# A fused transformer block on one core: down products three slots behind, and another order of the attention's steps

## The chip, the cores and the metric

The kernel runs on 1 core of one Trainium2 chip. The time is the device time in microseconds (us) of one launch, the median of 3 runs. A profiled execution of its own gives the trace; its time stands below beside the span of the trace. The engines are called PE (TensorE), DVE (VectorE), ACT (ScalarE), POOL (GpSimd) and SP (SyncE, which here only starts transfers).

## The reference

Four residual steps on x of 16 batches of 128 tokens by 128 features, in fp32:

```python
x = x + diffusion(x, zX, zY, zR)                    # two 3-point laplacians and zR * x * (1 - x)
x = x + moe(x, probs, shared_prob, Wg, Wu, Wd, Sg, Su, Sd)
#   8 dense experts and a shared one, F = 512: down(silu(x @ Wg) * (x @ Wu)), weighted by the batch's gates
x = x + lora(x, language_ids, A, B, embed)          # rank 16
x = x + attention(x, side, lengths, Wq..., bo)
#   16 heads of 8; 128 keys of the side input under a length mask, and one key of the token's own
```

## The kernel before, in words

**First phase: the experts.** The 16 batches are done in 4 tiles of 4 batches, so that a tile is 128 features by 512 tokens. A tile has 36 **slots**: 9 experts (the shared one is the ninth) by 4 chunks of 128 of the 512 hidden units. Slot k is: `gate_product` (g_ps), `up_product` (u_ps), and `down_product` of an earlier slot into acc_ps, which sums over all 36. Each product is three 128x512 matmuls (line 520 to 522), since every fp32 operand is split into a high and a low fp32r part: high by high, high by low, low by high. Between up and down the chunk goes through four steps: `silu` on ACT (act_p from g_ps, line 818), `product` on DVE (act_p times u_ps, line 1097), `round_act` on ACT (act_hi, line 823), `split_act` on DVE (act_lo = act_p - act_hi, line 1101). The order on each engine is written out by hand. ACT's slot k is silu of k, then round of k - 1; DVE's is product of k, then split of k - 1; PE's is gate of k, up of k, an auxiliary step if the slot has one, down of k - 2. act_p, act_hi and act_lo have three buffers each; g_ps and u_ps three banks each, so that gate k waits for silu k - 3 and up k for product k - 3.

The gates are applied to the input of the up product: for each expert POOL makes xg (line 1299) and xg_lo (line 1303), ACT xg_hi (line 828). In the first tile the weights are loaded and split too: SP loads w_raw (three buffers, three parts per expert), ACT rounds it (line 789), POOL subtracts (line 1292). **Auxiliary steps** lie in fixed slots of PE and drain on DVE or ACT one slot later. `FIRST_SLOT` lists those of the first tile: bias in slot 4, setup (two small transposes of the lora matrices) in 5, side in 6, query in 8, four natural projections in 10 to 16, and the next tile's from 18 on. A natural step has a product on POOL (`multiply_self`, line 1308, one slot later) and a sum on DVE (`sum_self`, line 1061, two slots later). After a query step SP writes q_rows to memory in six transfers of 128 KB, on the same queue as the weights. `add_experts` (line 1106) adds acc_ps to x1 in slot 1 of the next tile, and `later_step` runs lora, key and value for the tile before. The last tile's later steps are done in the first bodies of the attention.

**Second phase: the attention**, one `body` per batch b, in pairs of batches whose blocks SP loads (`load_first`: k_blocks and q_plain; `load_second`: q_blocks and k_plain; about 768 KB each). The scores are computed twice: `scores` (s_ps, queries on partitions), only to take each token's maximum on DVE (`max_group`, line 1169, then `merge_max`, line 1177); and `scores_t` (st_ps, keys on partitions) for the exponentials on ACT (line 931), where the maximum goes in as two extra rows of q_blocks. The maximum gets there in this way: POOL's `split_max` (lines 1360 to 1365) makes neg_max, PE's `turn_max` (line 595) transposes it, ACT's `copy_max` (line 883) copies it to max_rows, and POOL's `place_max` (line 1351) starts a transfer into q_blocks, which `scores_t` waits for. Then `weigh` (probabilities by values), `take_pv` on ACT, `turn_pv`, `normalise` on DVE, `turn_attn`, `copy_attn` on ACT, `project`, `make_out` on DVE, and the store on SP, one transfer per pair. PE's body b is, in this order:

```python
for i in range(2):
    scores(b + 2, n + 2, i)
    scores_t(b, n, i)
weigh(b - 1, n - 1, 0); weigh(b - 1, n - 1, 1)
turn_attn(b - 2, n - 2)
scores(b + 2, n + 2, 2); scores(b + 2, n + 2, 3)
scores_t(b, n, 2)
weigh(b - 1, n - 1, 2); weigh(b - 1, n - 1, 3)
project(b - 2, n - 2)
scores_t(b, n, 3)
turn_pv(b - 1, n - 1)
turn_max(b + 2, n + 2)
```

SP's `step(p)` starts load_first of pair p + 2, then load_second of pair p + 1 once the maximum of batch 2p + 1 is placed (`max_placed[1]`), then the store of pair p - 3; before step 2 it stores the k_rows of the last tile.

## Time and profile before

| | us |
|---|---|
| median of 3 runs | 474.82 |
| lowest, highest | 471.68, 476.14 |
| the profiled execution's own time | 470.62 |
| its span, first to last instruction | 468.8 |
| PE busy | 432.4 |
| DVE, ACT, POOL busy | 334.4, 282.0, 185.5 |

The profiled execution took 1.8 us more than its span, and 4.2 us less than the median. The span has these stretches: up to 8.07 the start; 8.07 to 113.87 the first tile, with the weights; 113.87 to 370.80 the three other tiles; from there the attention, in which 370.80 to 399.01 holds bodies 0 to 3 with the last tile's later steps, and 454.46 to 468.80 the last two bodies and the end. Matmuls are pipelined, and the profile models their ends: two that start 0.23 us apart are each shown as 0.39 us long. So a late start of less than 0.16 us does not show as idle time.

### The profile page before, as it was taken

The numbers are of one execution on the slowest core, as the hardware profiler recorded it, in microseconds if no ns is written. First come the engines' busy times: TensorE is split into PE (matmuls) and PEld (weight loads), VectorE is DVE, ScalarE is ACT, GpSimd is POOL, SyncE is SP. The second block draws the span as 40 slices with busy tenths as digits, with TensorE's granted clock in tenths as the row PEclk, the third lists the DMA queues.
The fourth block names the chain that finished last, engine by engine and source line by source line (L and its number), as shares of the span: only waits on it lengthen the run. The fifth ranks groups of instructions, "written<-read, shape, count | busy, mean of one in ns | idle before, by whom it ended". The sixth has DMA issues, their size and how long they took to land.

```text
span 468.8 us, 7759 instructions
## 1 busy us (share of the span) xinstructions
PE 432.4 (92%) x2280; PEld 324.5 (69%) x2280; DVE 334.4 (71%) x589; ACT 282.0 (60%) x572; POOL 185.5 (40%) x235
## 2 busy tenths in 40 slices
PE   7799699699999999999999999999999977988896
PEld 3568578578678787867878787788788554554453
DVE  4887467586777779777767987686687757567763
ACT  5757367575465657645565755555555646567684
POOL 0857567573223222332224222334377324234440
PEclk9999799899999999999999999999999989789999
DMA  5524214210002020000111000001221714665630
GB/s 161 157 74 149 91 52 129 78 37 3 1 1 90 1 68 1 22 0 0 53 36 35 32 0 1 1 27 42 69 70 34 171 50 122 175 156 148 152 104 24
DMA packets 27891, 30.69 MB, mean 65 GB/s; under 512 B 4276, under 2 KB 22296, under 8 KB 27864
## 3 DMA queue, kind: packets, MB, share of 16 engines
q1 hardware_dynamic: 26664, 29.99, 22.5%
q0 software_dynamic: 768, 0.28, 0.3%
q8 instruction: 12, 0.20, 0.2%
q10 hardware_dynamic: 432, 0.10, 0.1%
q14 instruction: 15, 0.12, 0.1%
HBM read 22.73 MB, written 7.35 MB: 64 GB/s over the span
## 4 chain that ended last, share of the span: by engine, by line
PE 59%; DVE 14%; issue 9%; DMA 6%; ACT 6%; POOL 5%; POOLq 1%; DVEq 0%; ACTq 0%; SPq 0%
PE acc_ps L520 7%; DVE act_lo L1101 6%; PE g_ps L520 5%; PE acc_ps L521 5%; PE g_ps L522 5%; PE g_ps L521 5%; PE acc_ps L522 5%; PE u_ps L520 5%; PE u_ps L522 5%; PE u_ps L521 5%; DVE act_p L1097 4%; DMA w_raw<-in_L_cond_Wu 4%; ACT act_p L818 2%; DMA squares<-in_squares 1%; DMA q_blocks<-max_rows 1%
## 5 line engine op out<-in xcount | busy, mean ns | idle before, releaser
L818 ACT ACTIVATE act_p<-g_ps 128x512 f32<-128x512 f32 x144 | 86.0, 597 | 127.9 <-PE g_ps L522 112.4
L1097 DVE TENSOR_TENSOR act_p<-act_p,u_ps 128x512 f32<-128x512 f32 x144 | 98.5, 684 | 71.4 <-PE u_ps L522 45.7
L1101 DVE TENSOR_TENSOR act_lo<-act_p,act_hi 128x512 fp32r<-128x512 f32 x144 | 122.8, 853 | 0.2 <-ACT act_hi L823 0.2
L1303 POOL TENSOR_TENSOR xg_lo<-xg,xg_hi 128x512 fp32r<-128x512 f32 x35 | 49.6, 1418 | 155.1 <-ACT xg_hi L828 155.1
L823 ACT ACTIVATE act_hi<-act_p 128x512 fp32r<-128x512 f32 x144 | 89.8, 624 | 2.0 <-DVE act_p L1097 1.8
L520 PE MATMUL acc_ps<-act_hi,w_split 128*128 128x512 f32 x144 | 62.0, 431 | 15.9 <-DVE act_lo L1101 15.8
L520 PE MATMUL g_ps<-x_hi,w_split 128*128 128x512 f32 (+1 forms) x144 | 57.6, 400 | 0.6 <-DVE x_lo L1130 0.6
L521 PE MATMUL acc_ps<-act_lo,w_split 128*128 128x512 f32 x144 | 57.1, 397 | 0.0
L522 PE MATMUL acc_ps<-act_hi,w_split 128*128 128x512 f32 x144 | 56.9, 395 | 0.0
L520 PE MATMUL u_ps<-xg_hi,w_split 128*128 128x512 f32 x144 | 56.8, 394 | 0.1
L521 PE MATMUL g_ps<-x_lo,w_split 128*128 128x512 f32 (+1 forms) x144 | 56.8, 394 | 0.0
L522 PE MATMUL g_ps<-x_hi,w_split 128*128 128x512 f32 (+1 forms) x144 | 56.8, 394 | 0.0
L521 PE MATMUL u_ps<-xg_lo,w_split 128*128 128x512 f32 x144 | 56.7, 393 | 0.0
L522 PE MATMUL u_ps<-xg_hi,w_split 128*128 128x512 f32 x144 | 56.6, 393 | 0.0
L1292 POOL TENSOR_TENSOR w_split<-w_raw,w_split 128x512 fp32r<-128x512 f32 x26 | 38.1, 1469 | 34.6 <-ACT w_split L789 34.6
L520 PEld LDWEIGHTS acc_ps<-act_hi,w_split 128*128 128x128 f32 x144 | 27.4, 190 | 34.1 <-DVE act_lo L1101 22.1
L1169 DVE TENSOR_REDUCE max_key<-s_ps 128x4 f32<-128x512 f32 x56 | 36.6, 686 | 16.2 <-PE s_ps L588 15.6
L1299 POOL TENSOR_TENSOR xg<-x,gates 128x512 f32 (+1 forms) x35 | 39.2, 1121 | 5.0 <-ACT x L798 2.8
L688 PE MATMUL st_ps<-q_blocks,k_plain 98*128 98x512 f32 x64 | 29.8, 471 | 3.5 <-DMA q_blocks<-max_rows 3.0
L520 PEld LDWEIGHTS g_ps<-x_hi,w_split 128*128 128x128 f32 x144 | 27.4, 190 | 7.1 <-DVE x_lo L1130 1.4
L520 PEld LDWEIGHTS u_ps<-xg_hi,w_split 128*128 128x128 f32 x144 | 27.3, 190 | 6.6 <-issue 0.5
L522 PEld LDWEIGHTS acc_ps<-act_hi,w_split 128*128 128x128 f32 x144 | 27.5, 191 | 6.1
(190 smaller groups left out, 679.8 us busy)
## 6 DMA issues: line engine op xcount, KB each, us to landing
k_blocks<-k_rows SPq DMA_DIRECT2D x32, 96.0 KB
q_plain<-q_rows SPq DMA_DIRECT2D x8, 384.0 KB
q_blocks<-q_rows SPq DMA_DIRECT2D x32, 96.0 KB
k_plain<-k_rows SPq DMA_DIRECT2D x8, 384.0 KB
w_raw<-in_L_cond_Wg SPq DMA_DIRECT2D x8, 256.0 KB, 2.7
w_raw<-in_L_cond_Wu SPq DMA_DIRECT2D x8, 256.0 KB, 2.7
w_raw<-in_L_cond_Wd SPq DMA_DIRECT2D x8, 256.0 KB, 2.9
q_rows<-rows_hi SPq DMA_DIRECT2D x16, 128.0 KB
```

Of the source, the lines that this page charges most:

```text
L520: mm(dst, w_h, x_h, start=start, stop=False)
L521: mm(dst, w_h, x_l, start=False, stop=False)
L522: return mm(dst, w_l, x_h, start=False, stop=stop)
L688: mm(st_ps[i % 2][:], k_plain[n // 2 % 2][0:ROWS + 2, i, half(n)], q_blocks[n // 2 % 2][0:ROWS + 2, :, i, half(n)], start=True, stop=True) ...
L818: activation(act_p[k % 3][:], g_ps[k % 3][:], ACT.Silu).then_inc(silu_done, 1)
L823: activation(act_hi[k % 3][:], act_p[k % 3][:], ACT.Identity).then_inc(act_hi_done, 1)
L1097: tt(act_p[k % 3][:], act_p[k % 3][:], u_ps[k % 3][:], ALU.mult).then_inc(prod_done, 1)
L1101: tt(act_lo[k % 3][:], act_p[k % 3][:], act_hi[k % 3][:].bitcast(F32), ALU.subtract).then_inc(act_lo_done, 1)
L1169: nc.vector.tensor_reduce(max_key[n % 2][:, i], (s_ps[i % 2] if bank is None else bank)[:].rearrange("p (j s) -> p j s", j=GJ), AX_X, ALU. ...
L1292: tt(w_lo[:, w // 3, w % 3], w_raw[w % 3][:], w_hi[:, w // 3, w % 3].bitcast(F32), ALU.subtract)\
L1299: tt(xg[:], x1[:, t], over_s(gates[:, e, bass.ds(t * TB, TB)]), ALU.mult).then_inc(xg_made, 1)
L1303: tt(xg_lo[e % 3][:], xg[:].rearrange("p b s -> p (b s)"), xg_hi[e % 3][:].bitcast(F32), ALU.subtract)\
```

## The change

Two things, and a few moves that go with them.

**Experts.** Down products lie three slots behind (`BEHIND = 3`) in place of two. act_hi and act_lo get four buffers (`ACTS = 4`), and act_p lies in the same memory as act_lo, so that `split_act` works in place; `silu` of k now waits for down k - 4 in place of split k - 3. `add_experts` moves from slot 1 to slot 2. In the first tile setup moves from slot 5 to slot 17; `sum_self` comes four slots after its natural step in place of two, and POOL's `multiply_self` at the start of the second slot in place of the end of the first. `select_language`, a small copy, is taken out of `later_step` to ahead of its wait. In the last slot of the last tile ACT rounds 34 before silu 35, and DVE splits 34 before product 35.

**Attention.** The body has both next scores first, then `turn_max(b + 1)`, then both transposed scores. `turn_max` of a batch is thus in the body after the one that took its maximum. ACT's `copy_max` and `exp_self` move along to the start of the body, and POOL's `place_max` comes ahead of `weigh_self`, with `pick_mask` ahead of it. A `first_body` mixes the last three down products with the first scores. The last two bodies have values, take_pv and copy_attn on DVE in place of ACT. The last pair is stored as two transfers; the other stores are where they were.

```diff
-FIRST_SLOT = {4: ("bias", 0, 0), 5: ("setup", 0, 0), 6: ("side", 0, 0), 8: ("query", 0, 0)}
+FIRST_SLOT = {4: ("bias", 0, 0), 6: ("side", 0, 0), 8: ("query", 0, 0)}
+FIRST_SLOT |= {17: ("setup", 0, 0)}
+ACTS = 4
+BEHIND = 3
...
-        act_p = [sb(f"act_p{n}", [128, N]) for n in range(3)]
-        act_hi = [sb(f"act_hi{n}", [128, N], F32R) for n in range(3)]
-        act_lo = [sb(f"act_lo{n}", [128, N], F32R) for n in range(3)]
+        act_hi = [sb(f"act_hi{n}", [128, N], F32R) for n in range(ACTS)]
+
+        with ExitStack() as products:
+            act_p = [products.enter_context(nc.sbuf_tensor(f"act_p{n}", [128, N], F32)) for n in range(ACTS)]
+        act_lo = [sb(f"act_lo{n}", [128, N], F32R) for n in range(ACTS)]
...
-                if p >= 3:
-                    store_out(p - 3)
+                if 3 <= p < NP + 2:
+                    store_out((p - 3) * PAIR, (p - 2) * PAIR)
...
+            for b in range(B - PAIR, B):
+                store_out(b, b + 1)
...
-                down_product(*((t, k - 2) if k >= 2 else (t - 1, SLOTS - 2 + k)))
+                down_product(*((t, k - BEHIND) if k >= BEHIND else (t - 1, SLOTS - BEHIND + k)))
...
+            def first_body():
+
+                down_product(NT - 1, SLOTS - 3)
+                pe.wait_ge(silu_done, NT * SLOTS - 1)
                 for i in range(2):
-                    if s_next:
+                    scores(2, 2, i)
+                down_product(NT - 1, SLOTS - 2)
+                pe.wait_ge(silu_done, NT * SLOTS)
+                for i in range(2):
+                    scores_t(0, 0, i)
+                down_product(NT - 1, SLOTS - 1)
+                for i in range(2, GI):
+                    scores(2, 2, i)
+                last_tile_step(0, 1)
+                scores_t(0, 0, 2)
+                last_tile_step(0, 2)
+                scores_t(0, 0, 3)
+
+            def body(b, n, s_next=True, turn_next=True):
+
+                if s_next:
+                    for i in range(2):
                         scores(b + 2, n + 2, i)
+                if turn_next:
+                    turn_max(b + 1, n + 1)
+                for i in range(2):
                     scores_t(b, n, i)
...
-                if s_next:
-                    turn_max(b + 2, n + 2)
...
             def silu(t, k):
-                wait(act, act_lo_done, t * SLOTS + k - 2)
+                wait(act, down_done, t * SLOTS + k - 3)
...
             def round_act(t, k):
-                wait(act, down_done, t * SLOTS + k - 2)
+                wait(act, down_done, t * SLOTS + k - 3)
...
-            def body(b, n, s_next=True):
+            def body(b, n):
+                if n:
+                    copy_max(b + 1, n + 1)
                 exp_scores(b, n, 0)
+                if n:
+                    exp_self(b + 1, n + 1)
                 exp_scores(b, n, 1)
...
-                for kind, f, b in first_at(k - 2):
+                for kind, f, b in first_at(k - 4):
                     if kind == "natural":
                         sum_self(f, b)
...
-                if k == 1:
+                if k == BEHIND - 1:
                     add_experts(t - 1)
...
+            def last_body(b):
+                place_values(b, b)
+                copy_attn(b - 2, b - 2)
+                take_pv(b - 1, b - 1)
+                make_out(b - 2, b - 2)
+                normalise(b - 1, b - 1)
...
             def pick_mask(b, n):
-                nc.gpsimd.tensor_copy(mask_col[n % 4][:], mask_cols[:, bass.ds(b, 1)]).then_inc(mask_picked, 1)
+                pool.wait_ge(max_copied, b + 1)
+                tt(mask_col[n % 4][:], mask_cols[:, bass.ds(b, 1)], warm[:, 0:1], ALU.add).then_inc(mask_picked, 1)
...
-            def body(b, n, s_next=True):
+            def body(b, n, s_next=True, place_next=True):
+                if n and place_next:
+                    pick_mask(b + 1, n + 1)
+                    place_max(b + 1, n + 1)
+                weigh_self(b, n)
                 if s_next:
                     split_max(b + 2, n + 2)
```

## Rows read from the trace of the kernel before

**Rows 1.** Windows by stage: stretch, length, busy times, granted clock, DMA share, GB/s.

```profile
8.07:113.87 105.80, 92.61 (x398) 72.45 (x399) 76.72 (x137) 67.00 (x128) 66.22 (x54) 0.95 0.31 90
113.87:200.13 86.26, 85.12 (x386) 68.62 (x385) 66.13 (x103) 50.95 (x95) 25.09 (x24) 1.00 0.08 25
...
370.80:399.01 28.21, 21.99 (x169) 12.89 (x167) 19.38 (x40) 15.89 (x39) 9.47 (x32) 0.93 0.38 98
399.01:454.46 55.45, 49.13 (x460) 29.01 (x460) 38.22 (x89) 37.72 (x99) 19.23 (x67) 0.91 0.57 152
```

**Rows 2.** Waits of PE, whole span: total us, times, longest us.

```profile
PE acc_ps L520 <- DVE act_lo L1101: 15.8, 17, 3.9
PE max_ps L595 <- POOL neg_max L1363: 7.7, 11, 2.9
PE st_ps L688 <- DMA q_blocks<-max_rows: 3.0, 3, 2.0
```

**Rows 3.** Timeline of PE, first tile: start, length, instruction, [idle before, releaser].

```profile
51.35 0.39 PE L522 MATMUL u_ps<-xg_hi,w_split 128*128 128x512 f32 x1
55.59 0.80 PE L520 MATMUL acc_ps<-act_hi,w_split 128*128 128x512 f32 x1 [3.86 <-DVE act_lo L1101]
...
91.00 0.54 PE L520 MATMUL acc_ps<-act_hi,w_split 128*128 128x512 f32 x1 [3.73 <-DVE act_lo L1101]
```

**Rows 4.** Timeline of the other engines in the first long wait.

```profile
51.36 0.63 ACT L789 ACTIVATE w_split<-w_raw 128x512 fp32r<-128x512 f32 x1 [3.78 <-DMA w_raw<-in_L_cond_Wu]
...
53.72 1.27 POOL L1303 TENSOR_TENSOR xg_lo<-xg,xg_hi 128x512 fp32r<-128x512 f32 x1
53.78 0.38 DVE L1061 TENSOR_REDUCE self_score<-stage 128x16 f32<-128x128 f32 x1 [5.01 <-POOL stage L1308]
```

**Rows 5.** Windows of the first tile with a granted clock of 0.50.

```profile
53.80:60.60 6.80, 5.01 (x12) 3.99 (x13) 4.60 (x10) 2.98 (x6) 4.05 (x4) 0.50 0.23 77
91.40:94.70 3.30, 3.30 (x9) 2.47 (x8) 3.30 (x7) 1.46 (x4) 1.13 (x2) 0.50 0.27 79
```

**Rows 6.** Timeline of PE, second tile: down products of three slots that follow one another.

```profile
129.64 0.39 PE L520 MATMUL acc_ps<-act_hi,w_split 128*128 128x512 f32 x1
...
131.68 0.39 PE L520 MATMUL acc_ps<-act_hi,w_split 128*128 128x512 f32 x1
...
134.12 0.51 PE L520 MATMUL acc_ps<-act_hi,w_split 128*128 128x512 f32 x1 [0.24 <-DVE act_lo L1101]
```

**Rows 7.** Timeline of DVE there: the split for the third of them.

```profile
132.51 1.56 DVE L1101 TENSOR_TENSOR act_lo<-act_p,act_hi 128x512 fp32r<-128x512 f32 x1
```

**Rows 8.** Timeline of PE from the last down products to the last tile's key.

```profile
368.91 0.50 PE L520 MATMUL acc_ps<-act_hi,w_split 128*128 128x512 f32 x1 [0.78 <-DVE act_lo L1101]
...
378.10 0.39 PE L595 MATMUL max_ps<-squares,neg_max 128*32 128x128 f32 x1 [2.87 <-POOL neg_max L1363]
...
380.90 0.63 PE L522 MATMUL out_ps<-in_hi,w_qkv_l 128*128 128x512 f32 x1
```

**Rows 9.** Timeline of PE in the loop of the attention.

```profile
427.73 0.28 PE L595 MATMUL max_ps<-squares,neg_max 128*32 128x128 f32 x1 [0.49 <-POOL neg_max L1363]
...
434.29 0.49 PE L688 MATMUL st_ps<-q_blocks,k_plain 98*128 98x512 f32 x1 [0.41 <-DMA k_plain<-k_rows]
...
438.89 0.28 PE L595 MATMUL max_ps<-squares,neg_max 128*32 128x128 f32 x1 [0.58 <-POOL neg_max L1363]
...
443.73 0.28 PE L595 MATMUL max_ps<-squares,neg_max 128*32 128x128 f32 x1 [0.49 <-POOL neg_max L1363]
```

**Rows 10.** Timeline of POOL and of SP there, and max_rows' tile view, last line.

```profile
429.23 0.63 POOL L1351 DMA_DIRECT2D q_blocks<-max_rows  x1
...
428.28 1.52 SPq L454 DMA_DIRECT2D q_blocks<-q_rows  x4
429.84 0.35 SPq L458 DMA_DIRECT2D k_plain<-k_rows  x1
...
DMA to landing us min/median/max: 2.3/3.9/7.1
```

More of the change, by code:

```diff
@@ L627, in down_product @@
                 pe.wait_ge(act_lo_done, t * SLOTS + k + 1)
-                last = three(acc_ps[:], w_hi[:, e, 2, chunk], w_lo[:, e, 2, chunk], act_hi[k % 3][:], act_lo[k % 3][:],
+                last = three(acc_ps[:], w_hi[:, e, 2, chunk], w_lo[:, e, 2, chunk], act_hi[k % ACTS][:], act_lo[k % ACTS][:],
                              start=(k == 0), stop=(k == SLOTS - 1))
@@ L677, in _ @@
                     turn_max(EARLY_TURN[k], EARLY_TURN[k])
-            for k in range(2):
-                down_product(NT - 1, SLOTS - 2 + k)
             def scores_t(b, n, i):
@@ L751, in body @@
                     turn_pv(b - 1, n - 1)
[L752 to L755 removed]
+            first_body()
             body(1, 1)
@@ L886, in last_slots @@
                 for k in range(LAST_ROUND, SLOTS):
-                    silu(t, k)
-                    round_act(t, k - 1)
+                    if k == SLOTS - 1 and not rounds_next:
+                        round_act(t, k - 1)
+                        silu(t, k)
+                    else:
+                        silu(t, k)
+                        round_act(t, k - 1)
                     if k == LAST_ROUND and rounds_next:
@@ L970, in body @@
                 exp_scores(b, n, 3)
-                if s_next:
-                    copy_max(b + 2, n + 2)
-                    exp_self(b + 2, n + 2)
+            def last_body(b):
+                if b + 1 < B:
+                    copy_max(b + 1, (b + 1) % TB)
+                exp_scores(b, b, 0)
+                if b + 1 < B:
+                    exp_self(b + 1, b + 1)
+                for i in range(1, GI):
+                    exp_scores(b, b, i)
             exp_self(0, 0)
@@ L1198, in slot @@
                         first_step(*step)
-                    for kind, f, b in next_at(k - 2, t + 1):
+                    for kind, f, b in next_at(k - 4, t + 1):
                         if kind == "natural":
                             sum_self(f, b)
-                product(t, k)
-                split_act(*((t, k - 1) if k else (t - 1, SLOTS - 1)))
-                if k == 1:
+                if isinstance(t, int) and k == SLOTS - 1:
+                    split_act(t, k - 1)
+                    product(t, k)
+                else:
+                    product(t, k)
+                    split_act(*((t, k - 1) if k else (t - 1, SLOTS - 1)))
+                if k == BEHIND - 1:
                     add_experts(t - 1)
@@ L1223, in _ @@
                         split_max(b, b)
+            max_group(2, 2, 0)
             split_act(NT - 1, SLOTS - 1)
+            max_group(2, 2, 1)
+            select_language(NT - 1)
             add_experts(NT - 1)
@@ L1262, in body, with last_body @@
                     normalise(b - 1, n - 1)
-            body(0, 0)
+            def last_body(b):
+                place_values(b, b)
[3 more added lines that the diff above has]
+                normalise(b - 1, b - 1)
+            max_group(2, 2, 2)
+            last_tile_step(0, 1)
+            max_group(2, 2, 3)
+            merge_max(2, 2)
+            last_tile_step(0, 2)
+            split_input(NT - 1)
             body(1, 1)
@@ L1316, in _ @@
                 e, c = divmod(k, FC)
+                for kind, f, b in first_at(k - 2):
+                    if kind == "natural":
+                        multiply_self(f, b)
                 if e + 1 < NE and c == 1:
@@ L1322, in _ @@
                     split_part(3 * (e + 1) + c)
-                for kind, f, b in first_at(k - 1):
-                    if kind == "natural":
-                        multiply_self(f, b)
                 for kind, f, b in first_at(k + PICK_AHEAD):
```

83 lines of the change are left out of this document (44 added, 39 removed).

## The prediction

> **What bounds the kernel now.** I read the windows by stage first, then the waits of PE, then the timelines where the waits lie. PE is busy in 85.12 of the 86.26 us of the second tile at a granted clock of 1.00, against 92.61 of 105.80 in the first tile at 0.95, 21.99 of 28.21 in the handover and 49.13 of 55.45 in the next ten bodies, at 0.93 and 0.91 [rows 1]. So PE sets the pace in the tiles and there is little to win in three of the four; the first tile and the attention are where it stands still. The waits say for whom: 15.8 us in 17 waits for act_lo before a down product, 7.7 us in 11 waits for neg_max before turn_max, 3.0 us in 3 waits for the placed maxima [rows 2]. The first two are what the change addresses.
>
> Two of the 17 waits are long, 3.86 and 3.73 us [rows 3]. At the first of them ACT waits 3.78 us for the weights of an up product, which come late behind the stores of q_rows; then POOL splits them, multiplies the natural step's product and makes xg_lo (53.72 to 54.99), and DVE stands 5.01 us at the sum of that product, with the product and the split that PE needs queued behind it [rows 4]. After both long waits the clock is at half, 1.2 of 2.4 GHz: PE is busy 5.01 and 3.30 us at 0.50 [rows 5]. The other waits are short. In the second tile two down products lie 2.04 us apart, which is a slot without an auxiliary step; the next comes after 2.44 [rows 6], since its split took 1.56 us [rows 7]. Of these 0.40 us the profile shows 0.24 as a wait; 0.16 is hidden by the modelled ends.
>
> **Experts: the short waits.** 15.8 less 7.6 leaves 8.2 us in 15 waits [rows 2, 3]; the last, 0.78 [rows 8], belongs to the handover. A further slot gives each split 2.04 us more, against a mean of 0.53, so all 14 should go: 7.4 us, and 14 times the hidden 0.16, 2.2 us, together 9.6. Not all is kept. The first ones lie in slots 2 to 4, where the next thing late is the input of the second expert's up product on POOL, which no change touches; I take off 1.6 (of some 3 us there), which leaves **8.0**. The bounds are 5, if those of the first tile turn into others, and 10.
>
> **The long waits.** The weights' landing stays. PE gets one gate product more done meanwhile (a third of a slot, 0.68 us), then up k + 1 waits for xg_lo, which ends at 54.99 where the down product waited until 55.59 [rows 3, 4]: 0.6 us. So each long wait gives 1.28, the two **2.5**; that sum_self is later only frees DVE, which is then not the last. Nothing at all and 4 us are the ends, the latter if the stores come earlier than the weights by more than PE does. The waits that are left are 2 to 3 us.
>
> **The clock in the first tile.** 8.3 busy us at half cost 4.2 us [rows 5]. Whether waits of 2 to 3 us still end in half clock no row says: those of 3.86 and 3.73 did, the wait of 2.87 in the handover too [rows 3, 8]. I take **1.0**, with 0 and 4.2 as ends. The Trainium skill ("TensorE: Matmul & The Clock Gate", Part 1) says that the halved clock is the default and that a PE left idle falls back to it, so that shorter gaps should save more than their own length; by that rule the term would be 4.2. The trace agrees on the direction only.
>
> **What the experts' part adds.** PE has the same products. silu k waits for down k - 4, which stands ahead of gate k in PE's own order, so this wait never ends last, nor does that of round_act. Four buffers cover three products in flight and one being made. add_experts is in slot 2: the sum is now needed at slot 3 by lora and by down 0, as it was at slot 2 by down 0, so the same 0.2 us at most is late, and 0.7 if the longer split [rows 7] falls just ahead of it. Behind it on DVE stands product 3, which PE needs three slots on. Setup in slot 17 costs the two transposes that slot 5 saves. The copy ahead of lora's wait is covered by that wait. All this is 0, with 2 us of loss at the end of its range.
>
> **The handover.** Now the maxima of batch 2 are merged behind the lora steps on DVE; PE stands 2.87 us for neg_max at 378.10, 0.78 at the down products, and runs the key products at half clock until 380.90 plus a matmul [rows 8]. With the new order the four scores of batch 2 lie between the last down products, so the maxima are done earlier, and the turn comes two scores later. Next late is the input of the key product (lora, add, round, split in a row), by about 1 us. The waits of 3.65 go down by that 1, and split 35 is some 0.7 later behind a max_group: **2.0**, with 0 and 3.7 (with the clock) as ends.
>
> **The loop.** From turn to turn a body without a wait for transfers takes 4.84 us, 0.49 of it the wait for neg_max [rows 9]. In the new order two scores (0.5 us) cover that, but DVE's normalise, started by turn_pv, now stands between PE and the next maxima, and scores 3 of the body meet it: I take 4.5 per body. But the loop has a second bound, the transfers. place_max is issued 1.50 us after the turn [rows 9, 10], lands after 3.9 [rows 10], SP then issues q_blocks (1.6 to k_plain), and k_plain, issued at 429.84, is awaited at 434.29, 4.4 us later [rows 9, 10]: 11.4 us from a turn to the transposed scores that are two bodies on. That is why pairs take over 2 x 4.84: in 55.45 us there are five, 11.1 each [rows 1]. The change brings the issue to about 1.0 after the turn, since own_w no longer stands ahead of it: 0.5 less per pair on that path. So a pair gives 0.5 where the transfers bind and 0.7 where PE does; I take 0.55, for the five pairs and the half pair before them **3.0**. Ends: -6 and +6. The last two bodies lose three ACT steps each to an idle DVE, but have the placement of the last maximum closer; no row prices it and I take **0.5**, from -1 to 1.5. Both stores of the last pair: 0.
>
> **Sum.** 8.0 + 2.5 + 1.0 + 2.0 + 3.0 + 0.5 = 17.0. The profiled execution took 470.62, so 453.6; from the median of 474.82 it is 457.8. Terms that overlap (a wait that goes in the first tile is there again at the next DMA) make me round up to **459**, 3.3% less.
>
> **Rivals.**
> 1. *The transfers take back the attention's part.* With shorter bodies the 3.9 us of a placement [rows 10] leave no room, and every wait for neg_max returns as a wait for q_blocks or k_plain. For it: DMA engines are at a share of 0.57 there [rows 1], and the chain of 11.4 us is already binding. Against it: the placement is issued sooner. Then only the experts and the handover gain, 13.5 less some 3: 474.8 - 10 = 465.
> 2. *The clock comes back in full.* All half-clock stretches shrink with the gaps (4.2 us in the first tile; in the ten bodies the mean is 0.91 [rows 1], 5 us at most): 459 - 6 = 453. This is the result that the skill's rule above would give.
> 3. *In the first tile the waits only move.* PE, a slot ahead, waits for xg_lo or w_split in place of act_lo, all along and not only at the long waits; POOL is busy 66.22 of 105.80 us there [rows 1], which is its highest share in any stage, but with room. Experts give 4, attention 4: 467.
> 4. *Slower.* One mechanism: a placement is now issued in the very body before its scores, while SP's loads of a pair start. Let L be its landing. A body can't be shorter than L + 0.8. With the 3.9 of the median that is 4.7; it costs more than the experts bring once L is over 5.5 in most bodies, and with 6 (the longest is 7.1 [rows 10]) twelve bodies at 6.8 in place of 5.3 are 18 us, less 12: 481. In the last two bodies alone there is something more: DVE now copies the values from SBUF to SBUF. The Trainium skill ("SBUF — State Buffer", SBUF: two separate sides) says that a transfer issued from GpSimd can't get its descriptors written while VectorE runs such an fp32 copy; by that rule one landing, the last, would be late by the length of the two copies, and no row of before shows it, since the copies were on ACT.
> 5. *It doesn't do what it says*: the long waits set the first tile whatever lies between, and the half clock moves to other slots. Within 1% of 474.8.
>
> **Chances.** Forecast (455 to 463) 0.50; rival 1, 0.21; rival 2, 0.11; rival 3, 0.08; rival 4, 0.04; rival 5, 0.06. The range has to leave out no more than 0.2: the slower case, the nothing, and tails. It goes from 452 (rival 2 and the high ends) to 468 (rival 3). About 1%, 4.7 us, is what a measurement of this kernel can tell from no change, since three runs of it lie 4.5 us apart. Faster by over 1%: the forecast and rivals 1 to 3, less a little, 0.88; within 1% 0.08; slower 0.04.
>
> **What would show it.** PE's waits for act_lo should go from 15.8 us to under 2, and in their place the first tile should have two waits before an up product, of 2 to 3 us, for xg_lo. The first tile should be 6 to 9 us shorter than 105.80, the second about 1 us shorter than 86.26. The waits of max_ps for neg_max should be gone in the loop; waits of st_ps for DMA should be there still, 0.3 to 1 us each at every second body. A body without such a wait should take 4.5 and not 4.84, and the placement should be issued 1.0 and not 1.50 us after the turn. The key's last product should end some 2 us closer to the last down product. The prediction is wrong if waits of act_lo stay, if POOL's splits of weights are what PE waits for in the first tile, if the attention from 370.80 on takes as long as now, 98 us, or if the half-clock stretches grow.

## The result, and the profile after

The changed kernel takes **458.63 us** (median of 4, 455.09 to 467.31) against 474.12 us of the kernel before in the same comparison (4 runs, 471.68 to 476.14): ratio 0.965, 95% interval 0.956 to 0.975. The medians here are over all executions; the ratios leave disturbed ones out, so that the two don't always divide exactly. The profiled execution took 456.68 us with a span of 454.9, against 470.62 and 468.8 before.

Windows of the kernel after, by the same stages as [rows 1] (first tile, second tile, handover, ten bodies; stretch, length, busy times of PE, PEld, DVE, ACT, POOL, granted clock, DMA share, GB/s):

```profile
8.07:107.50 99.43, 90.33 (x391) 72.62 (x392) 76.23 (x135) 66.45 (x127) 65.91 (x53) 0.95 0.32 96
107.50:191.34 83.84, 83.69 (x383) 68.47 (x382) 66.23 (x103) 51.18 (x95) 23.98 (x23) 1.00 0.09 26
...
359.27:382.48 23.21, 19.70 (x165) 11.27 (x164) 18.30 (x38) 14.69 (x38) 8.98 (x32) 1.00 0.38 103
...
382.48:439.55 57.07, 50.64 (x458) 29.27 (x459) 37.27 (x91) 37.75 (x100) 21.02 (x71) 0.85 0.56 153
```

Read the lengths against [rows 1]. The start of the second tile is 113.60 before and 107.50 after, so the first tile gives 6.1 us; up to the end of the last tile it is 11.5 (370.77 to 359.27). The handover gives 5.0 (28.21 to 23.21). In the new order four of its matmuls lie ahead of that edge (165 in the stretch, 169 before); at 0.23 us each they move 0.9 us from one account to the other, so for the same work the tiles give some 12.4 and the handover some 4.1. The ten bodies that follow are **1.6 us longer** (55.45 to 57.07), and the rest, up to the end of the span, 1.0 longer (14.34 to 15.35). -11.5 - 5.0 + 1.6 + 1.0 is -13.9, the difference of the spans. The second tile has 0.15 us of idle PE left, where [rows 1] show 1.14: nothing is to be had there any more. Its window in [rows 1] begins and ends one or more matmuls late (386 of them, where the tile has 383). From first gate product to first gate product it is 85.71 us before, and so 1.87 longer than after:

```profile
113.60:199.31 85.71, 84.57 (x383) 68.14 (x382) 65.58 (x103) 50.95 (x95) 24.53 (x23) 1.00 0.08 25
```

Waits of PE after, to be set beside [rows 2]:

```profile
PE u_ps L526 <- issue: 7.4, 3, 2.9
PE st_ps L692 <- DMA k_plain<-k_rows: 3.9, 3, 1.5
...
PE st_ps L692 <- DMA q_blocks<-max_rows: 1.5, 1, 1.5
PE s_ps L594 <- DMA q_plain<-q_rows: 1.5, 1, 1.5
...
PE aux_ps L533 <- DVE own_values L1062: 0.8, 1, 0.8
...
PE max_ps L601 <- POOL neg_max L1440: 0.2, 1, 0.2
```

The 15.8 us for act_lo are gone altogether, and of the 7.7 us for neg_max 0.2 are left. In their place stand three waits before up products of the first tile (7.4 us), and waits for data from DRAM in the attention (6.9 us for k_plain, q_plain and the placed maxima). The view names nothing for the three, but each ends 0.1 us after POOL's xg_lo, as the prediction said of two of them:

```profile
51.85 1.27 POOL L1380 TENSOR_TENSOR xg_lo<-xg,xg_hi 128x512 fp32r<-128x512 f32 x1
53.22 0.77 PE L526 MATMUL u_ps<-xg_hi,w_split 128*128 128x512 f32 x1 [2.35 <-issue]
```

In the two later ones POOL itself stood first, for weights that ACT had waited for (3.62 and 3.87 us); the first, at 20.94, has POOL's own work ahead of it and no late transfer.

Where the clock is at half after, three stretches of the first tile and three of the attention:

```profile
22.16:25.58 3.42, 3.42 (x10) 2.75 (x9) 3.42 (x5) 1.28 (x3) 2.71 (x3) 0.50 0.27 79
52.88:56.30 3.42, 3.08 (x8) 2.53 (x9) 2.54 (x5) 1.34 (x3) 3.42 (x4) 0.50 0.10 32
87.02:90.43 3.41, 3.39 (x10) 2.38 (x9) 3.41 (x8) 2.36 (x7) 1.40 (x3) 0.50 0.26 77
383.98:387.39 3.41, 3.41 (x24) 2.06 (x23) 1.69 (x4) 1.93 (x6) 0.80 (x4) 0.50 0.54 175
394.22:401.04 6.82, 5.29 (x41) 2.63 (x38) 2.66 (x5) 2.89 (x8) 1.28 (x3) 0.50 0.55 154
418.11:424.94 6.83, 6.75 (x45) 4.25 (x46) 2.12 (x6) 3.64 (x9) 1.71 (x6) 0.50 0.73 189
```

The three of the first tile hold 9.89 busy us of PE, where [rows 5] hold 8.31; the three in the ten bodies hold 15.45, where two stretches of before (6.82 and 3.41 us long, at 398.53 and 412.18) hold 9.75. At half clock each busy us costs up to half a us, so the ten bodies pay up to 7.7 us after and 4.9 before. Each of the six begins beside a wait of PE: at most 0.4 us before its end, at most 1.5 us behind it (the waits end at 20.94, 53.22, 86.17, 382.48, 393.76 and 418.19). The reverse does not hold: the experiments show the same waits without half clock behind them.

Timeline of PE after, in the loop, with the turns of the maxima (compare [rows 9]):

```profile
402.49 0.27 PE L601 MATMUL max_ps<-squares,neg_max 128*32 128x128 f32 x1
...
406.95 0.27 PE L601 MATMUL max_ps<-squares,neg_max 128*32 128x128 f32 x1
...
411.40 0.27 PE L601 MATMUL max_ps<-squares,neg_max 128*32 128x128 f32 x1
...
418.19 1.22 PE L692 MATMUL st_ps<-q_blocks,k_plain 98*128 98x512 f32 x2 [1.40 <-DMA k_plain<-k_rows]
...
425.16 0.27 PE L601 MATMUL max_ps<-squares,neg_max 128*32 128x128 f32 x1
```

The first three turns are 4.46 and 4.45 us apart, a body in which nothing is late: it was 4.84 [rows 9]. The wait for k_plain at 418.19 and the half clock behind it make the body from 416.51 (the turn ahead of it) to 425.16 one of 8.65 us. It is 4.2 us longer than a short one, about what ten short ones save against before (10 times 0.39).

### The profile page after: what moved, and what is told of

Same layout as the page of the kernel before. It is cut to its first block, busy times and chain, and to the rows that moved or that the text cites. A ratio compares the mean times of both kernels' runs of the same rounds, so it can differ in the third digit from the quotient of the medians.

```text
span 454.9 us, 7748 instructions
## 1 busy us (share of the span) xinstructions
PE 427.5 (94%) x2280; PEld 326.0 (72%) x2280; DVE 336.1 (74%) x598; ACT 279.9 (62%) x563; POOL 185.5 (41%) x235
## 4 chain that ended last, share of the span: by engine, by line
PE 75%; DMA 10%; DVE 5%; issue 3%; ACT 3%; POOL 2%; SPq 1%; DVEq 0%; ACTq 0%; POOLq 0%
PE acc_ps L526 7%; PE u_ps L526 6%; PE acc_ps L528 6%; PE acc_ps L527 6%; PE g_ps L526 6%; PE g_ps L528 6%; PE g_ps L527 6%; PE u_ps L528 6%; PE u_ps L527 6%; DMA w_raw<-in_L_cond_Wu 4%; DMA k_plain<-k_rows 3%; PE pv_ps L702 3%; PE st_ps L692 2%; DMA q_blocks<-max_rows 2%; PE s_ps L594 2%
## 5 line engine op out<-in xcount | busy, mean ns | idle before, releaser
L526 PE MATMUL acc_ps<-act_hi,w_split 128*128 128x512 f32 x144 | 59.0, 410 | 0.0
L528 PE MATMUL acc_ps<-act_hi,w_split 128*128 128x512 f32 x144 | 56.9, 395 | 0.0
L1207 DVE TENSOR_REDUCE max_key<-s_ps 128x4 f32<-128x512 f32 x56 | 36.1, 684 | 12.4 <-PE s_ps L594 11.9
L692 PE MATMUL st_ps<-q_blocks,k_plain 98*128 98x512 f32 x64 | 28.8, 487 | 7.1 <-DMA k_plain<-k_rows 3.9
L526 PEld LDWEIGHTS acc_ps<-act_hi,w_split 128*128 128x128 f32 x144 | 27.2, 189 | 8.6 <-issue 3.4
L526 PEld LDWEIGHTS g_ps<-x_hi,w_split 128*128 128x128 f32 x144 | 27.4, 190 | 6.9 <-DVE x_lo L1168 1.4
L528 PEld LDWEIGHTS g_ps<-x_hi,w_split 128*128 128x128 f32 x144 | 27.3, 190 | 6.0
```

The costliest lines, as they stand in the source:

```text
L526: mm(dst, w_h, x_h, start=start, stop=False)
L528: return mm(dst, w_l, x_h, start=False, stop=stop)
L692: mm(st_ps[i % 2][:], k_plain[n // 2 % 2][0:ROWS + 2, i, half(n)], q_blocks[n // 2 % 2][0:ROWS + 2, :, i, half(n)], start=True, stop=True) ...
L1207: nc.vector.tensor_reduce(max_key[n % 2][:, i], (s_ps[i % 2] if bank is None else bank)[:].rearrange("p (j s) -> p j s", j=GJ), AX_X, ALU. ...
```

## The experiments

**The two halves apart.** The first kernel has the experts' part in the old attention, the second the attention's part over the old experts.

```diff
# experts only (before, with)
+ACTS = 4
+BEHIND = 3
-            for k in range(2):
-                down_product(NT - 1, SLOTS - 2 + k)
+            for k in range(BEHIND):
+                down_product(NT - 1, SLOTS - BEHIND + k)
...
# attention only (after, with)
-ACTS = 4
-BEHIND = 3
+ACTS = 3
+BEHIND = 2
...
-                down_product(NT - 1, SLOTS - 3)
```

> The experts' part alone (down products three slots behind, four buffers, setup in slot 17, sums later) with the attention in its order of before. My theory: all of the first phase's gain comes from it. The trace of the changed kernel ended its last down product 11.5 us earlier; here too it should be 11 to 12 us earlier, and the attention from there on as long as before (98 us in the trace). In all 10 to 13 us less than before, some 461 to 464. Rival (the attention's order is the larger part, and the first phase moved by chance of the clock): 3 to 6 us less than before.

> The attention's part alone (new order, first body, last bodies) with down products two slots behind and three buffers as before. My theory: what it gains lies in the handover, about 5 us up to the transposed scores of batch 4, and of these 1 to 3 us are given back in the loop to waits for transfers: 1 to 4 us less than before in all, 470 to 473. Rival (the loop's part was lost only to a half clock that came by chance): 7 to 9 us less than before. Second rival (the loop is slower by itself in the new order): no gain or a loss.

Measured: experts only 461.23 us (ratio 0.977, 0.971 to 0.983), attention only 469.22 (0.994, 0.989 to 0.998), both against a before of 473.34. The first is inside its 461 to 464. The second is 0.8 us under its 470 to 473, but by its ratio 3.0 us less than before, inside the 1 to 4 of its theory. In the trace of the first the last tile ends at 359.86, 10.9 us sooner than before, and the attention then takes 99.9 us, where before takes 98.0. The handovers of the two, in windows (the attention's part was profiled in an execution of 473.56 us, 4.3 over its median; this stretch is at full clock):

```profile
359.86:388.75 28.89, 22.83 (x169) 13.69 (x167) 19.53 (x40) 15.92 (x39) 9.51 (x32) 0.88 0.35 92
```

```profile
371.30:394.44 23.14, 19.68 (x165) 11.29 (x164) 18.25 (x38) 14.89 (x38) 8.93 (x32) 1.00 0.43 109
```

28.89 us with the old order and 23.14 with the new one, against 28.21 [rows 1] and 23.21: the handover's 5 us, with the 0.9 of the moved edge in them, belong to the attention's order alone, whatever the experts do. What follows: the halves add up (2.3% and 0.6% are 2.9%; together they gave 3.5%, interval 2.6 to 4.4), and the attention's order is worth 3 us alone by its ratio and 1.2% on top of the experts, where the intervals of the two (0.971 to 0.983 and 0.956 to 0.975) overlap. Alone it is less than the 5 us of the handover: part of these is lost again later.

**The loads made small.** From the third pair on every load of blocks and of the plain rows moves one row, and from the rows of an earlier pair, so that the scores are computed from other data; the engines' instructions stay. The same edit in both kernels.

```diff
-                    r = slice(3 * DH * j, 3 * DH * (j + 1))
+                    r = slice(3 * DH * j, 3 * DH * j + (3 * DH if p < 2 else 1))
...
+                rows = ROWS if p < 2 else 1
+                sp.dma_start(dst[0:rows].bitcast(F32).rearrange("r i n -> r (i n)"),
```

> The changed kernel, but from pair 2 on the loads of a pair's blocks move one row per transfer, from the rows of pairs 0 and 1 (so the attention of later batches is computed on rows of earlier ones): as many transfers and waits, hardly any bytes. If transfers bind the loop, as I think, the ten bodies from the transposed scores of batch 4 to those of 14, 57.1 us in the changed kernel, fall to ten times the body without a wait, 4.45 us: 44 to 46 us. If the engines bind it (rival), they stay above 53 us.

> The kernel of before with the same light loads (later batches computed on rows of pairs 0 and 1). Ten bodies, 55.5 us in before, fall to 10 times 4.84, 48 to 49 us, if transfers bind. The difference to the light changed kernel is then what the new order is worth where no transfer is late: 3.5 to 4.5 us in ten bodies by my theory; 0 by the rival that DVE's normalise takes the place of the wait for neg_max.

Measured: 446.67 us with the new order and 466.6 with the old one, one execution each. The loop in windows, from the transposed scores of batch 4 to the turn ten bodies on, first the new order, then the old one:

```profile
382.55:429.46 46.91, 44.31 (x458) 25.48 (x458) 36.28 (x87) 36.95 (x99) 20.25 (x69) 1.00 0.12 33
```

```profile
398.92:450.08 51.16, 45.47 (x458) 27.38 (x459) 37.59 (x88) 37.71 (x98) 19.42 (x69) 0.97 0.10 28
```

With full loads the same stretch takes 55.87 us in the new order (382.48 to 438.35) and 55.11 in the old one (399.01 to 454.12). Both came out a little above what was expected (44 to 46 and 48 to 49 us); the difference was expected at 3.5 to 4.5. So the new order is worth 4.25 us (51.16 - 46.91) when data are there in time: 36.08 us for eight bodies, 4.51 each, against 45.2 for nine, 5.02 each. But the transfers cost the new order 9.0 us and the old one 4.0, and that takes all of it back. By PE's busy time in these windows (44.31 and 45.47 us light, 50.36 and 48.84 full) 6.05 of the 9.0 and 3.4 of the 4.0 are the same 458 matmuls taking longer at half clock, and only the rest is idle time. PE was at full clock all through the new order's stretch, where it had three half-clock stretches with full loads, though waits of 1.61 and 1.78 us ended at its start and in it (382.55 and 388.89). So the full loads are the cause of the loop's miss, shown from both sides; how it splits into waits and clock is one execution's account, since the clock behind a wait changes from one to the next (below).

**Which property of the transfers.** Two edits to SP's order of the loads of a pair. One lets q_blocks and k_plain start without the wait for the placed maximum; the other starts k_plain ahead of that wait.

```diff
# early loads
-                    sp.wait_ge(max_placed[1], PLACED * (p + 1))
                     load_second(p + 1)
...
# k_plain early
+                    m = (p + 1) % 2
+                    load_plain(k_plain[m], k_rows, p + 1, second_loaded[m])
                     sp.wait_ge(max_placed[1], PLACED * (p + 1))
-                    load_second(p + 1)
+                    load_blocks(q_blocks[m], q_rows, p + 1, second_loaded[m])
```

> The changed kernel with the loads of q_blocks and k_plain started as soon as their buffers are free, without SP's wait until the maximum of batch 2p + 1 is placed. My theory: the long waits for k_plain (1.4 to 1.5 us at every second body) come from that chain of placement, landing and loads; they go, and waits for the placed maxima come up in their place, since a placement now shares the engines with 768 KB more. Net between 2 us faster and 3 us slower than the changed kernel, 457 to 462. Rival (the bytes bind, not the chain): the waits for k_plain stay where they are and the time is the same.

> The changed kernel with only k_plain (half of the bytes of that load) started early, q_blocks still behind the placement. My theory: waits for k_plain go, placements land 0.5 us later, and bodies of a pair's start come close to 4.5 us: 1 to 4 us faster than the changed kernel, 455 to 458. Rival (placements are what is late in any case): waits for q_blocks take their place, and the time stays at 459.

Measured: 460.18 us (ratio 0.958, 0.952 to 0.965) and 455.36 (0.963, 0.959 to 0.967); the intervals overlap with that of the change, 0.956 to 0.975, and both medians lie inside what was expected (457 to 462 and 455 to 458). The six executions of the first edit lie between 451.84 and 465.20 us, wider than those of any other kernel here, so little can be read from its time. The prediction held a chain of 11.4 us responsible (placement, its landing, the issue of q_blocks, then k_plain's landing). The first edit cuts it, and this is PE's timeline in it:

```profile
376.31 0.73 PE L691 MATMUL st_ps<-q_blocks,k_plain 98*128 98x512 f32 x2 [2.30 <-DMA q_blocks<-max_rows]
...
387.98 0.70 PE L691 MATMUL st_ps<-q_blocks,k_plain 98*128 98x512 f32 x2 [2.56 <-issue]
...
401.54 0.73 PE L691 MATMUL st_ps<-q_blocks,k_plain 98*128 98x512 f32 x2 [1.91 <-DMA q_blocks<-max_rows]
...
414.39 0.70 PE L691 MATMUL st_ps<-q_blocks,k_plain 98*128 98x512 f32 x2 [2.61 <-issue]
```

No wait for k_plain is left, and 11.5 us of waits for the placement or for nothing named have come (3 and 3 of them), against 6.9 for transfers after the change. The small placement now shares the queues with the large loads: it lands after 4.2 us in the median, where it took 3.6. The time hides this: the profiled execution took 457.49 us against 456.68, but its first tile, the same program, ended 2.5 us sooner (105.05 against 107.50), and its attention took 3.3 us longer. So the wait that ends last changes its name with each order and doesn't get shorter. With k_plain alone ahead the waits for k_plain are gone too, and 4.3 us for q_blocks and the placed maxima and 3.5 us without a name stand in their place (in an execution of 461.22 us); that it goes first helps a little at most.

**The stores of the first tile.** SP issues the six stores of q_rows in a row, ahead of the weights of an up product. Here each goes out one slot after another.

```diff
-                    first_store(*step)
+                    spread_store(*step)
+                store_one()
```

> The changed kernel with the six stores of q_rows in the first tile one per slot, in place of six ahead of the next weights. My theory: the two waits of 2.5 to 3 us before an up product come only from these stores; they go, and with them the half clock behind them. 4 to 7 us faster than the changed kernel, 452 to 455, and the first tile 5 to 7 us shorter. Rival (the loads of weights are slow then for another reason, or POOL, at 66 of 99 us in that stage, is next late at once): less than 2 us.

Measured: **450.49 us**, ratio 0.954 (0.949 to 0.959), faster than the 452 to 455 that was expected. SP's timeline of the change, and then with spread stores:

```profile
35.95 2.58 SPq L395 DMA_DIRECT2D q_rows<-rows_hi  x4
38.57 1.41 SPq L395 DMA_DIRECT2D q_rows<-rows_lo  x2
40.02 1.61 SPq L375 DMA_DIRECT2D w_raw<-in_L_cond_Wu  x1
```

```profile
36.62 0.68 SPq L418 DMA_DIRECT2D q_rows<-rows_hi  x1
38.39 0.34 SPq L375 DMA_DIRECT2D w_raw<-in_L_cond_Wu  x1
```

The weights' issue alone takes 1.61 us behind the six stores and 0.34 otherwise, and it starts 1.6 us sooner. The first tile in windows with it:

```profile
8.07:99.93 91.86, 85.68 (x392) 69.32 (x392) 78.88 (x135) 66.28 (x127) 66.86 (x53) 1.00 0.36 104
```

99.43 us have become 91.86: two of the three waits for an up product are gone and the clock stays at full. The last tile ends at 351.73, 7.5 us sooner than after the change, which is more than the whole gain of the profiled pair (6.4). This doesn't hang on one trace: with the experts' part and the six stores in a row the second tile starts between 105.05 and 108.47 us in six kernels, with spread stores between 99.42 and 99.95 in five. The 99.42 belongs to the one of the five that has a half-clock stretch in that tile. The loop is unchanged in kind: three waits for k_plain of 5.6 us in all.

The full clock is not what the gain hangs on. The wait at 20.94, which no store touches, is still there, just as long, and the stretch that was at half clock after the change is at full:

```profile
20.96 0.47 PE L543 MATMUL u_ps<-xg_hi,w_split 128*128 128x512 f32 x1 [2.14 <-issue]
```

```profile
22.16:25.58 3.42, 3.42 (x17) 2.85 (x16) 3.42 (x4) 2.71 (x5) 2.70 (x3) 1.00 0.27 79
```

And half clock there can be free. From the third wait to the second tile, first after the change and then in the kernel with small loads, whose first tile is the same program:

```profile
86.17:107.50 21.33, 20.43 (x88) 16.29 (x89) 18.97 (x32) 14.49 (x29) 12.51 (x10) 0.92 0.09 26
```

```profile
86.22:107.53 21.31, 18.95 (x88) 15.26 (x89) 18.96 (x32) 14.28 (x29) 12.51 (x10) 1.00 0.09 26
```

At full clock PE is busy 1.5 us less and waits as much longer, for own_values on DVE. Behind the second wait it seems to have cost something: 32.95 us (53.22 to 86.17, with half clock) against 30.95 in the first edit of the loads (52.81 to 83.76, without).

**The auxiliary moves undone.** Setup back in slot 5, the sum of the natural step's product two slots behind it, the product at the slot's end, as before; all else as after.

```diff
-                for kind, f, b in first_at(k - 4):
+                for kind, f, b in first_at(k - 2):
```

> The changed kernel with setup back in slot 5, sum_self two slots after its natural step and multiply_self at the end of the slot: only the down products' distance and the buffers are left of the experts' part. My theory: the moves matter only where PE would wait for DVE, in slots 4 to 6 and at the natural steps. There DVE stood 5.0 us at the sum, and with it in the queue the act_lo that the down product needs is later than xg_lo again: 1 to 3 us slower than the changed kernel, 459.5 to 462. Rival (the further slot covers it all): no difference.

Measured: 459.91 us, ratio 0.974 (0.969 to 0.979). The second tile starts at 107.24 and the last ends at 359.00, as after (107.50 and 359.27), though the waits lie elsewhere: the longest for an up product is 3.7 us, where the change has 2.90. So these moves show no worth in the first phase; since the same first tile scattered by 2.6 us between kernels, one or two us of it would not be seen. The time lies inside the theory's 459.5 to 462, but the trace speaks for the rival. The ratio's interval overlaps that of the change a little; in the trace the difference lies in the attention (98.9 us against 95.6), where both kernels have the same instructions. That it is chance is argued, not shown.

**SP's order put together.** Spread stores with k_plain early; spread stores with the last tile's six k_rows stores also taken apart, two at a time among the loads; the spread stores with the experts' part and the old attention; and the first three edits together.

```diff
# last tile's keys
-                    later_stores(NT - 1)
...
+                if p in (2, 3):
+                    store_one()
+                    store_one()
```

> The spread stores of the run before, and in the attention SP issues k_plain ahead of its wait for the placed maximum. In the spread run the waits for k_plain were 5.6 us in 3. Theory A (the transfers are short of a few us of lead, and any lead helps): these waits fall to under 2 us, the placement's own waits stay at 3 to 4 us as in the run with k_plain early alone, and the time is 447 to 450, 1 to 3 less than with the spread stores alone. Theory B (the same bytes compete, so a load that starts earlier delays the placement by as much): the waits change their name from k_plain to q_blocks<-max_rows, and the time is 450 to 453, no gain.

> The spread stores, and the last tile's six k_rows stores, which took 4.8 us of SP in a row at 370 to 375 us ahead of the loads of pairs 4 and 3, now go two at a time: two ahead of these loads, two behind them, two later still. Theory A (the attention's transfers are late because of this block of stores): the loads of pair 3 are issued some 3 us sooner, the first k_plain wait of 2.6 us and the half clock around 382 and 392 us go, and the time is 446 to 449. Theory B (the steady loads bind, each pair for itself): the first wait goes or moves, the two later ones stay, half clock stays with them, and the time is 449 to 452.

> The spread stores with the experts' part of the change alone; the attention keeps the order of before. It asks what the attention's new order is worth once the first tile no longer stands still. If the order is worth what the comparison of the whole change with its experts' part alone says (0.3 to 1.2%), the time is 452 to 456 against 450.5 with both. If the order's gain is only the handover and the loop gives all of it back, 450 to 452. If the order gives its full 0.4 to 0.5 us per body here, 457 or more.

> All three edits of SP's order together: first tile's q_rows stores one per slot, last tile's k_rows stores two at a time, k_plain ahead of the wait for the placement. Alone with the first, the second gave 449.3 and the third 447.9 us. Theory A (they take away different waits: the block of stores at 370 us, and the late k_plain): the long stand of 4.0 us at 382 us goes, half clock behind it too, and the time is 444 to 446.5. Theory B (both only shift the same transfers): one wait of 2 us or more stays somewhere in pairs 3 to 6 and the time is 447 to 449.5.

Measured: 447.93 us (ratio 0.950, 0.945 to 0.955), 449.26 (0.950, 0.946 to 0.955), 453.50 (0.960, 0.955 to 0.964), and all together **445.60** (0.944, 0.940 to 0.949), the fastest kernel of this study, 5.6% under the kernel before. The last figure's interval lies clear of that of the change (0.956 to 0.975) and touches that of the spread stores alone in its last place. Of the other three none is apart from the spread stores alone (0.949 to 0.959) by its interval.

SP's timeline with spread stores only, at the pairs that follow the handover, then with the k_rows stores taken apart as well:

```profile
369.87 2.50 SPq L395 DMA_DIRECT2D k_rows<-rows_hi  x4
372.41 2.29 SPq L395 DMA_DIRECT2D k_rows<-rows_lo  x2
374.80 3.29 SPq L475 DMA_DIRECT2D k_blocks<-k_rows  x4
```

```profile
373.79 1.25 SPq L418 DMA_DIRECT2D k_rows<-rows_hi  x2
378.31 1.70 SPq L475 DMA_DIRECT2D k_blocks<-k_rows  x4
```

Six stores keep SP for 4.8 us, and the four loads behind them are issued in 3.29 us where they otherwise take 1.5 to 1.7. For k_plain early on top of the spread stores the first theory of its expectation gave 447 to 450 and the second 450 to 453; 447.93 is the first one's, but one stand of 4.0 us was left, at 382.40, that neither had. That stand became 1.7 us at 379.77 in the last kernel. There the first theory (444 to 446.5) came out in the time, while a wait of 2.19 us at 393.60 stayed, as the second had it, and so did half clock behind the stand (about 381 to 388). For the k_rows stores taken apart alone, 449.26 lies at the border of its two theories: the k_plain waits fell to 2.8 us, but those for the placement rose from 1.4 to 4.5, and the stretches of half clock moved. Ten bodies in windows, of that kernel and then of the last one:

```profile
378.29:431.62 53.33, 45.80 (x458) 26.22 (x458) 36.77 (x89) 37.02 (x99) 20.47 (x69) 0.97 0.62 162
```

```profile
373.50:428.82 55.32, 48.12 (x458) 27.96 (x457) 37.62 (x90) 37.53 (x100) 20.77 (x70) 0.91 0.62 157
```

Both are well over the 46.91 of the small loads, by 6.4 and 8.4 us. Of these 4.9 and 4.6 are idle time of PE (7.53 and 7.20 against 2.60), and 1.5 and 3.8 are busy time at half clock. The kernel with the old attention took 453.50 against 450.49: by the medians the new order is worth 3.0 us with this first tile as well, inside the 452 to 456 that the whole change's comparison gave, though the intervals overlap.

## Why the prediction was right

459 was forecast and 458.63 measured, inside the range and in the likeliest case. The sum behind it was right in its largest part, the experts' 11.5 us. It was too small in the handover and wrong in the clock, the loop and the end, and these errors nearly cancelled: that the time was met to 0.4 us is luck. One of its own signs of being wrong came true as well, since the half-clock stretches grew.

- *What bounds the kernel, and the experts' terms:* right. Forecast 8.0 + 2.5 + 1.0 = 11.5, measured 11.5 (12.4 for the same work). Of the parts, the long waits gave 2.3 (7.59 less 5.25, the last two of the three waits for an up product). The first tile gave 6.1, the others 1.9, 2.5 and 1.0, where about 1 was forecast for the second. The hidden share was larger than the 0.16 per wait: of the second tile's 1.87 us the three waits that the profile names are 1.10. The 1.6 that I took off for the first slots was right in kind and a little small: a wait of 2.14 at 20.94, for POOL's xg_lo, took the place of 1.18 and 1.80.
- *The clock in the first tile:* wrong in sign. I took +1.0 and the stretches at half grew from 8.31 to 9.89 busy us, which is up to 0.8 us lost. Waits of 2.14, 2.35 and 2.90 us each had half clock behind them in this execution. But the same first tile with small loads has it behind one of its three (2.14, 2.75 and 2.32), with spread stores it is at 1.00 throughout, the 2.14 included, and behind the third wait it cost nothing. So whether a wait of 2 to 3 us brings half clock is not decided by its length, and what I priced as half the busy time is an upper end. The rule of the Trainium skill ("TensorE: Matmul & The Clock Gate", Part 1) that an idle PE falls back agrees in direction; the result that I drew from it, that shorter gaps give all 4.2 us back, did not come.
- *The handover:* too small. 2.0 with an end of 3.7, measured 5.0, or 4.1 for the same work (and 23.14 us with the attention's part alone). PE's idle time fell from 6.22 to 3.51 us and its busy time from 21.99 to 19.70, of which the four moved matmuls explain 0.9 and the half-clock stretch of before at 378.05 the rest. The key's third product lies 7.61 us behind the last down product (358.27 to 365.88). Before it was 11.15, from 369.75 (the down product shown in [rows 8] is the last but one) to 380.90: 3.5 closer, where I said 2. First before, then after:

```profile
369.75 0.50 PE L520 MATMUL acc_ps<-act_hi,w_split 128*128 128x512 f32 x1
```

```profile
358.27 0.50 PE L526 MATMUL acc_ps<-act_hi,w_split 128*128 128x512 f32 x1
...
365.88 0.39 PE L528 MATMUL out_ps<-in_hi,w_qkv_l 128*128 128x512 f32 x1
```

- *The loop:* this is the step that failed. Forecast 3.0 gained, measured 1.6 lost. The PE side was right (4.5 per body forecast, 4.45 measured). The step "a pair gives 0.5 where the transfers bind" was not: I took a chain of issues, with a shorter link in it, for the bound. The link didn't shorten as said. The placement is issued 1.40 us after the turn, not 1.0, since the mask's copy waits for the same max_rows and 0.37 us more pass before the issue:

```profile
412.24 0.19 POOL L1448 TENSOR_TENSOR mask_col<-mask_cols,warm 128x1 f32<-128x1 f32 x1 [0.79 <-ACT max_rows L906]
412.80 0.65 POOL L1428 DMA_DIRECT2D q_blocks<-max_rows  x1 [0.37 <-issue]
```

  And cutting the chain gave nothing. What the small loads show in its place is that the bytes of the loads hold the loop up, by 9.0 us in the new order, of which 6.05 are half clock. That is the mechanism of rival 1, for the loop alone; its 465 did not come, because experts and handover gave 16.5 and not the 10 that it left them. That a wait would cost its own length and then the clock again was the range's end of +6 or -6, not a term of the sum, and it should have been one.
- *The last two bodies:* forecast 0.5 gained. From the transposed scores of batch 14 to PE's last product it is 11.27 us before and 11.10 after, so 0.2; the rest of the span got longer because the last store ended 3.4 us after DVE's last addition and not 2.2. The same instructions took 2.0 in three later kernels and 3.6 in the last one, so that part is the execution's.
- *Sum:* 17.0 forecast, 13.9 in the profiled pair, 15.5 between the medians. Handover +3.0, loop -4.6 and tail -1.5 against the forecast leave -3.1; the rounding up by 1.2 covered part, the scatter of the medians the rest.
- *Rivals 2 to 5* are out. Rival 2's half-clock stretches did not shrink. Landing of the placement: 3.6 in the median and 6.1 at most, so rival 4's 5.5 in most bodies was not near. DVE's two copies ran from 438.99 on, across the issue of the last placement at 439.17, and the transposed scores that need it started at 442.71 without a named wait: no delay shows here.

## What to carry to other kernels

A wait at an engine with a clock that can fall can be priced twice: once for its length and once for the half clock behind it. The second price is uncertain: here the same wait had it in one execution and not in another, and where PE would have waited again soon after, it cost nothing (21.33 against 21.31 us). Give it as a range. Where an order takes idle time out of a loop that is also fed by transfers, measure the loop once with the transfers made tiny: the difference says how much of the gain can arrive at all. And before a chain of issues is shortened, look at what one queue issues in a row: six small stores ahead of a load that is due cost this kernel more than the whole new order of its attention brought.

## What was not expected of the hardware

- **Stores lengthen the issue of the loads behind them.** On SP's queue a load of weights took 0.34 us to issue, 1.61 behind six stores; four loads of k_blocks took 1.52 us, and 3.29 right behind six stores.
- **The same wait, another clock.** In two of the last kernels PE does the same work from 350 to 357.4 us (5.84 and 5.79 busy us, at clocks of 1.00 and 0.99), with the same wait of 0.92 us for probs_t at 357.5. Behind it, first with the spread stores alone, then with the k_rows stores taken apart as well:

```profile
357.70:367.60 9.90, 9.57 (x102) 6.29 (x102) 7.91 (x16) 6.60 (x18) 3.34 (x10) 1.00 0.31 86
```

```profile
357.70:367.60 9.90, 9.90 (x59) 7.65 (x60) 4.35 (x8) 3.98 (x9) 1.97 (x7) 0.50 0.30 85
```

  The second did 59 matmuls where the first did 102, and was 4.1 us behind at the transposed scores of batch 2. So what brings half clock isn't settled by the last wait's length; what decides between the two was not found. The wait of 2.14 us in the first tile says the same: half clock stands behind it after the change, and full clock in all four traces with spread stores and the new attention. It also means that a single profile of the attention can be off by some 4 us, and that the loop's comparison rests on the small loads, where the clock was 1.00 and 0.97.
- **Open:** which share of the loop's late loads is bandwidth and which the order on the queues. The DMA share there is 0.56 to 0.62 in the mean, but in one-us windows it comes in bursts: after the change 9 of 58 are over 0.9, among them this one, and 7 are at 0.02 or less. No run separated the two.

```profile
424.00:425.00 1.00, 1.00 (x5) 0.83 (x4) 0.55 (x2) 0.69 (x1) 0.00 (x0) 0.53 1.09 184
```
